# Edge network, second pass: the gather written straight into the hidden layer's banks, in two column tiles

## What is computed

```python
D, H = 64, 64
for s in range(S):
    ce = jnp.concatenate([e, n[senders], n[receivers]], axis=-1)
    e = e + _ln(_mlp(ce, edge_blk_w0[s], edge_blk_b0[s], edge_blk_w1[s], edge_blk_b1[s]), g[s], beta[s])
    agg = jax.ops.segment_sum(e.astype(jnp.float32), receivers, num_segments=num_nodes)
    cn = jnp.concatenate([n, agg.astype(n.dtype)], axis=-1)
    n = n + _ln(_mlp(cn, ...), ...)
```

## Time and profile before

| | us |
|---|---|
| median of 3 runs | 20097.11 |
| lowest and highest | 20082.25, 20124.14 |
| the profiled execution | 20072.68 |
| its span, first to last instruction | 20070.7 |

### The profile page before, as it was taken

How to read it: one execution, slowest core, us unless ns; L and a number is a source line. 1 busy time by engine, 2 the same in 40 slices (tenths; PEclk the granted TensorE clock), 3 DMA queues, 4 the chain that set the end, 5 groups by cost and what they waited for, 6 DMA issues and landing times. The chain is left out here.

```text
span 20070.7 us, 577236 instructions
## 1 busy us (share of the span) xinstructions
PE 15562.4 (78%) x211534; PEld 14106.5 (70%) x211534; DVE 13897.1 (69%) x33414; ACT 8145.1 (41%) x17256; POOL 5737.8 (29%) x4543
## 2 busy tenths in 40 slices
PE   2666666666667996799999999996788888856665
PEld 1666666666654996788888888885677777746665
DVE  3777777777766996554555555554777777769999
ACT  0444444444442332455555555553344444421111
POOL 1888888888870110011111111110000000001111
PEclk9555555555556997899999999997899999977676
DMA  2222222222222552444444444442444444417676
GB/s 56 54 53 53 53 53 51 52 53 53 53 51 78 157 157 73 103 111 108 110 110 108 110 110 110 109 110 65 132 132 135 134 136 131 134 56 209 176 207 182
DMA packets 1403272, 2071.03 MB, mean 103 GB/s; under 512 B 764952, under 2 KB 938022, under 8 KB 1359282
## 3 DMA queue, kind: packets, MB, share of 16 engines
q1 hardware_dynamic: 1089098, 1709.41, 27.3%
q0 software_dynamic: 218240, 197.29, 8.9%
q10 hardware_dynamic: 94544, 142.53, 1.9%
HBM read 1521.71 MB, written 523.16 MB: 102 GB/s over the span
## 5 line engine op out<-in xcount | busy, mean ns | idle before, releaser
L759 POOL DMA_INDIRECT records<-e_sort_rec,e_sort_index x3300 | 4353.2, 1319 | 1064.0 <-issue 990.8
L2275 PE MATMUL e_s_ps_g<-e_s_parts,e_s_pick 128*128 128x64 bf16 x65340 | 2927.7, 200 | 760.4 <-DVE e_s_to_hot L1922 289.1
L2275 PEld LDWEIGHTS e_s_ps_g<-e_s_parts,e_s_pick 128*128 128x128 bf16 x65340 | 2679.7, 103 | 912.0 <-issue 599.7
L2280 PE MATMUL e_s_ps_g<-e_s_window,e_s_to_hot 128*128 128x64 bf16 x23100 | 1982.1, 199 | 25.8 <-issue 25.3
L1938 DVE COPY e_s_g_sb<-e_s_ps_g 128x512 f32<-128x512 f32 x880 | 605.7, 688 | 1847.8 <-PE e_s_ps_h L2298 1376.8
L2394 POOL DMA_DIRECT2D states<-e_s_second_t x550 | 475.0, 864 | 4919.1 <-ACT e_s_second_t L2134 4575.6
L1088 PE MATMUL e_sort_acc<-e_sort_thirds,e_sort_hot 128*128 128x48 f32 x7260 | 1574.7, 414 | 319.0 <-DVE e_sort_hot L918 319.0
L1088 PEld LDWEIGHTS e_sort_acc<-e_sort_thirds,e_sort_hot 128*128 128x128 f32 x7260 | 1557.0, 332 | 351.4 <-DVE e_sort_hot L918 351.4
L2385 POOL DMA_INDIRECT e_s_spill<-send,e_s_lists x220 | 243.5, 1107 | 4315.5 <-DMA e_s_window_in<-recv 4210.1
L2280 PEld LDWEIGHTS e_s_ps_g<-e_s_window,e_s_to_hot 128*128 128x128 bf16 x23100 | 1274.8, 102 | 28.4 <-issue 27.6
L1921 DVE TENSOR_SCALAR e_s_pick<-e_s_rows,lane_below 128x1024 bf16<-128x1024 bf16 (+1 forms) x3300 | 1243.2, 432 | 0.0
(11 more groups left out here) (540 smaller groups left out, 35769.6 us busy)
## 6 DMA issues: line engine op xcount, KB each, us to landing
e_s_rows<-rows_d SPq DMA_DIRECT2D x330, 1088.0 KB, 5.3
e_s_hot<-hots_d SPq DMA_DIRECT2D x550, 560.0 KB, 4.0
e_s_to_rows<-rows_d SPq DMA_DIRECT2D x220, 608.0 KB, 5.8
e_s_rows<-rows_d SPq DMA_DIRECT2D x220, 544.0 KB, 4.3
e_s_rows<-rows_d SPq DMA_DIRECT2D x220, 512.0 KB, 5.0
e_s_to_rows<-rows_d SPq DMA_DIRECT2D x220, 512.0 KB, 6.2
states<-e_s_first_t ACTq DMA_DIRECT2D x440, 256.0 KB, 2.5
states<-e_s_second_t POOLq DMA_DIRECT2D x440, 256.0 KB
```

The costliest lines, as they stand in the source:

```text
L759: pool.indirect_dma_start(records, bass.IndirectOffsetOnAxis(ap=index[x][:, t:t + 1], axis=0), rec[x][:, t, :], None,).then_inc(written[x] ...
L2275: pe.matmul(to_, pick[p][:, h, here], parts[:, SPAN * c + h, r, :], start=h == 0 and r == 0, stop=False)
L2280: mm = pe.matmul(to_, to_hot[p][:, here], window[:, r, 1, :], start=c == SPILL and r == 0, stop=r == 2)
```

## The change

In the second pass alone, the operands of the gather change places. The table (`parts` or `window`, 64 columns) is now stationary and the one-hot (128 slots of a cell, or up to four cells' receivers side by side) moves. The result comes out turned, 64 features on the partitions, so it is written directly into the hidden layer's bank: even cells into partitions 0 to 63, odd cells into 64 to 127, which are two column tiles of the array (the program gives these matmuls tile size 128x64 at positions 0,0 and 0,64). The hidden layer gets five banks, one per group, in place of two, and `ps_g` and `g_sb` are gone in this pass. With them go `gathered_` on VectorE and the turning matmuls of `hidden1`. The spilled rows are turned by one f32 matmul per block. `hidden1`, `act1_`, `out1` and `out1_` each stand one step earlier in the order. The indirect DMA for `spill` waits for the hidden layer of two blocks before in place of `gathered_`.

```diff
-        g_sb, act1 = tiles("g_sb", [LANES, 8 * D]), tiles("act1", [LANES, 512])
+        act1 = tiles("act1", [LANES, 512])
...
-        ps_g, ps_h1, ps_o1, ps_sum = ps("g", NB), ps("h1", NB), ps("o1", NB), ps("sum")[0]
+        ps_h1, ps_o1, ps_sum = ps("h1", NH), ps("o1", NB), ps("sum")[0]
+
+        def hidden_bank(s):
+            return ps_h1[0 if enc else s]
...
-                    if main and s:
+                    if enc and main and s:
                         gathered_(k - 1, y, s - 1, before - 1)
...
-                    if main and 2 <= s < NG + 2:
+                    if enc and main and 2 <= s < NG + 2:
                         act1_(k - 1, y, s - 2, before - 1)
-                    if main and s >= 3:
+                    if enc and main and s >= 3:
                         out1_(k - 1, y, s - 3, before - 1)
+                    if not enc and main and 1 <= s < NG + 1:
+                        act1_(k - 1, y, s - 1, before - 1)
+                    if not enc and main and 2 <= s < NG + 2:
+                        out1_(k - 1, y, s - 2, before - 1)
...
+            def gather_turned(k, x, s, before):
+                c0, e = PARTS5[s]
+                p = (x + s) % 2
+                halves = [hidden_bank(s)[half * D:(half + 1) * D, :] for half in range(2)]
+                pe.wait_ge(vp.sem, vp.at(f"to{s}", k))
+                if s == 0:
+                    pe.wait_ge(vx.sem, vx.end(k))
+                if before:
+                    pe.wait_ge(aH.sem, aH.at(f"{s}", k - 1))
+                to_pairs = to_hot[p][:, :].rearrange("p (j w l) -> p w j l", w=2, l=LANES)
+                for r in range(3):
+                    for half in range(2):
+                        n_ = (e - c0 + 1 - half) // 2
+                        pe.matmul(halves[half][:, 0:n_ * LANES], window[:, r, 1, :], to_pairs[:, half, 0:n_, :], start=r == 0, stop=False,
+                                  skip_group_check=True)
+                for j in pairs(s):
+                    mine = [(half, c0 + 2 * j + half) for half in range(2) if c0 + 2 * j + half < OWN]
+                    for h in range(SPAN):
+                        for r in range(3):
+                            for half, c in mine:
+                                mm = pe.matmul(halves[half][:, j * LANES:(j + 1) * LANES], parts[:, SPAN * c + h, r, :],
+                                               pick[p][:, h, (c - c0) * LANES:(c - c0 + 1) * LANES], start=False, stop=False, skip_group_check=True)
+                if e > OWN:
+                    j, half = divmod(OWN - c0, 2)
+                    for r in range(3):
+                        mm = pe.matmul(halves[half][:, j * LANES:(j + 1) * LANES], window[:, r, 0, :], to_hot[p][:, (OWN - c0) * LANES:(OWN - c0 + 1) * LANES],
+                                       start=False, stop=False, skip_group_check=True)
+                mm.then_inc(tg.sem, 1)
+
+            def hidden1_turned(k, x, s, before):
+                c0, p = PARTS5[s][0], (x + s) % 2
+                n_ = turned(s)
+                if s == NG - 1:
+                    j, half = divmod(SPILL - c0, 2)
+                    pe.wait_ge(spilled[x], block_of(k, x, 16))
+                    pe.matmul(hidden_bank(s)[half * D:(half + 1) * D, j * LANES:(j + 1) * LANES], spill[x][:, :], ident128[:, :], start=False, stop=False,
+                              skip_group_check=True)
+                pe.wait_ge(states_in[p], groups_of(k, x, s, 0))
+                mm = pe.matmul(hidden_bank(s)[:, 0:n_], W["eblk_e1"][:, :], states[p][:, 0:n_], start=False, stop=True, skip_group_check=True)
+                mm.then_inc(tH.sem, 1)
...
                     if main and s < NG:
-                        gather(k - 1, y, s, before - 1)
+                        (gather if enc else gather_turned)(k - 1, y, s, before - 1)
+                    if not enc and main and 1 <= s < NG + 1:
+                        hidden1_turned(k - 1, y, s - 1, before - 1)
...
-                    if main and s >= 3:
+                    if enc and main and s >= 3:
                         out1(k - 1, y, s - 3, before - 1)
+                    if not enc and main and 2 <= s < NG + 2:
+                        out1(k - 1, y, s - 2, before - 1)
...
                 if before >= 2:
-                    pool.wait_ge(vg.sem, vg.end(k - 2))
+                    pool.wait_ge(tH.sem, tH.end(k - 2))
```

More of the change, by code:

```diff
@@ L1751, in sorted_mlp @@
             attr_t = tile("attr_t", [LANES, 3 * LANES])
+            g_sb = tiles("g_sb", [LANES, 8 * D])
             act0, sq0 = tiles("act0", [LANES, 512]), tiles("sq0", [LANES, 8 * D])
@@ L1764, in sorted_mlp @@
         if enc:
-            ps_h0, ps_o0, ps_u, ps_w = ps("h0")[0], ps("o0")[0], ps("u")[0], ps("w")[0]
-        ps_g, ps_h1, ps_o1, ps_sum = ps("g", NB), ps("h1", NB), ps("o1", NB), ps("sum")[0]
+            ps_h0, ps_o0, ps_u, ps_w, ps_g = (ps(k)[0] for k in ("h0", "o0", "u", "w", "g"))
+        ps_h1, ps_o1, ps_sum = ps("h1", NH), ps("o1", NB), ps("sum")[0]
+        def hidden_bank(s):
+            return ps_h1[0 if enc else s]
         def inside(k):
@@ L2056, in body @@
                         var1(k - 1, y, 0)
-                if main:
+                if enc and main:
                     gathered_(k - 1, y, 4, before - 1)
@@ L2270, in gather @@
                     here = slice((c - c0) * LANES, (c - c0 + 1) * LANES)
[L2271 removed]
+                    to_ = ps_g[:, (c - c0) * D:(c - c0 + 1) * D]
                     if c < OWN:
```

24 lines of the change are left out of this document (9 added, 15 removed).

## The result

The change made the kernel faster, and by less than half of what the forecast said: 19861.65 us (median of four runs, 19815.21 to 19890.73) against 20098.17 for the kernel before on the same chip, ratio 0.9876 [0.9859, 0.9894], 237 us less. The forecast was 517 us less than the 20097 before.

The account below looks back on a forecast made before the run. The bound was taken to be a TensorE–VectorE ring over the last `out1`, `roots` and `picks(2)`. Ring 27.0 plus disturbances 1.1 gave 28.1 us per block, 4.5 less; over 110 blocks 495 us off, 19580 us, range 19410 to 20150.

Parts of the forecast that it names:

- The price of the gather: TensorE's gather: two neighbouring column tiles stream at once, 58.6 ns a pair, 2.77 us per group of eight cells.
- Loads half hidden: Rival for the gather: a tile's next load waits for its own stream, 86 ns a pair, 19790 us; chance 0.12.
- Loads exposed: Rival for the gather: both loads and the stream run in sequence, 113 ns a pair, 20125 to 20250 us; chance 0.05.
- One tile at a time: Rival for the gather: two column tiles do not stream together, 5.54 us per group, 20500 us; chance 0.11.
- The turnings and their copies: TensorE's turning matmuls go, 0.43 to 0.47 us per group of eight; VectorE loses four copies of 0.60 a block.
- The change of tile shape: TensorE entering and leaving column tiles five times a block: taken as nothing, upper bound 1.7 us a block.
- The clock: TensorE's granted clock in the second pass: 0.93 before, forecast to be above 0.93 after.
- half clock: Rival: the clock stays at the lower level through the gathers, over 40 us a block, some 21400 us; chance 0.03.
- What bounds the kernel now: Second pass: a ring `picks(2)`, gather, last `out1`, `roots`; 30.4 us undisturbed (TensorE 21.3, VectorE 9.1), 32.6 on average.
- The ring after: The same ring after the change: 18.5 us on TensorE plus 8.5 on VectorE, 27.0 us; 28.1 per block with disturbances.
- the sign by which one would see that its ring was wrong: Gather at its price but period not near 28, above all if VectorE waits elsewhere than `less0(3)` or `var1`.
- disturbances: Mean block period beyond the undisturbed turn, partly lower clock after waits: 2.2 us before, 1.1 taken for after.

Follow-up runs that it names:

- e5: The changed kernel, issuing all 36 gather matmuls of a group's even cells, then all 36 of the odd ones, instead of alternating; 20352 us.
- e7: e1 with `merge` one step later on VectorE, behind `picks(2)` and `norm1(1)`; 19460 us.
- e9: e7 with the spilled rows' matmul at the end of gather 4 and the `states` load for groups 0 and 1 ahead of `load_late`; 19345 us.
- e3: The changed kernel with `hidden1`, `act1_`, `out1` and `out1_` put back to their old steps; 19855 us.
- e6: e3 with `part0` and `part1` one step earlier on ScalarE; 19903 us.
- e11: e6 with `windows` and `picks(0)` ahead of `var1(1)` on VectorE; 19751 us.
- e1: The changed kernel with `part0` and `part1` one step earlier in ScalarE's order; 19491 us.

## Why the prediction was right in its direction and wrong in its size

- **The price of the gather: right.** A group of eight takes 2.67 us (0.66 + 2.01) against 2.77 forecast, a pair 56 ns against 58.6, and *Loads half hidden* (86 ns) and *Loads exposed* (113 ns) fell. By the rule of the Trainium skill behind the second, "TensorE: Matmul & The Clock Gate", The mechanism, loads that share their rows don't overlap; the trace doesn't agree, 27.9 ns a matmul leave no room for an uncovered load. *One tile at a time* fell too, and its price was right to some 8%: e5 brought it about at 54 ns a matmul.
- **The turnings and their copies: right.** Their rows are gone; `hidden1` stands directly behind the gather.
- **The change of tile shape, taken as nothing: a term of the wrong size.** An entry with its exit costs about 0.3 us (0.34 by e7 and e9), five of them some 1.5 us a block, near the upper bound of 1.7. The place that the forecast read its nothing from really shows none, and why it differs wasn't tried. By the rule of the Trainium skill, "TensorEngine Tiling (Array Packing)", Key Properties, a change of tiling mode drains the engine. The trace agrees as far as these gaps go; that they are a drain it does not show. They explain most of why gather 2 to the last second layer took 19.2 us and not 18.5. They also explain why TensorE's work came out above 25.3: that figure, with 0.1 less for each of four gathers and about 0.3 more for each of e9's four visits, comes near e9's 25.9.
- **The clock: right.** 0.98 after, 1.00 where TensorE waits little; "half clock" fell. In e3 and e6 a wait of some 3.2 us ahead of gather 2 stayed (269.5 us, 85 times, in e3 from 14300 to 16900 us), and with it a clock of 0.94.
- **"What bounds the kernel now" and "The ring after": wrong, and this is the step that failed.** The forecast closed the ring over the *last* `out1` and `roots`, because that interval and VectorE's part added up to the period. The numbers do add up, and so do those of the other way, over `out1(1)`, its square and VectorE's dense stretch; both come near 30.4 us. Rows that were there to be read tell them apart: VectorE waited for ScalarE in `less0(3)` and for `var1(1)` (130.4 us, 111 times) and then no more until `picks(2)`. Behind the last groups it was ScalarE's square that waited for VectorE (68.4 us, 109 times), so there VectorE was the late one and an earlier last `out1` could not help. The forecast put the ring through an edge at which its own waiting engine never waited. That the squares' edge is the binding one rests on e11, e6 and e1 together; no run lengthened it to see the period follow.
- **The step left out: ScalarE.** The forecast gave it one sentence, 13.7 us of work a block. It counted its load, not its order. `out1_` moved a step ahead of `part0` of the block before, and VectorE came to wait up to 4.2 us for it: 716 us of waits in the place of 207. e1 undoes this alone and gives 3.5 us a block. The text did name the sign by which one would see that its ring was wrong, the gather at its price and the period not near 28; but it looked above all for a wait in places other than `less0(3)`, and it was there, twice as long.
- **The direction: right in part by luck.** The forecast had 3.4 us a block from a shorter ring (30.4 to 27.0) and 1.1 from fewer disturbances. Measured, the undisturbed turn went from 30.4 to 30.04 us, 0.4 in place of 3.4, and the disturbances, the mean less that turn, from 2.2 to 0.6 us, 1.6 in place of 1.1. What the change gained by itself is mostly the smaller of the two terms.
- With that out of the way the kernel runs at 27.12 us a block, a little better than the 28.1 that the forecast had for the change. The 110 x 3.5 us between e1 and the change are what the forecast missed by, and more.

## What to carry to other kernels

When a step of one block is moved earlier in an in-order engine's program, everything of the other blocks that stands behind it is moved later: list, for each such instruction, who waits for it, however little the engine is loaded. When a ring is closed to explain a period, check each of its edges for who is late there; a sum that matches the period is met by more than one ring. Two half-width tiles want their matmuls issued in turn, one of each, and as few entries and exits as the order allows.
